# The window mask moved from matrix products to VectorE, the maximum's subtraction to GpSimd, and a new order on every engine

## The reference

```python
q, k, v = x @ Wq + bq, x @ Wk + bk, x @ Wv + bv      # 16 query heads of 8, 2 key/value heads
# keys padded by 16 on both sides; each block of 32 queries sees a span of 64 keys
scores = einsum('bhntd,bhnud->bhntu', qb, kb)         # 32 queries x 64 keys
win_mask = (u >= t) & (u < t + 32)
scores = where(win_mask, scores, -inf)
probs = softmax(scores, axis=-1)
out = einsum('bhntu,bhnud->bhntd', probs, vb)
...
x = x + out @ Wo + bo
```

## Time and profile before

| | us |
|---|---|
| median of 3 runs | 632.43 (631.92 to 635.89) |
| the profiled execution itself | 634.98 |
| its span, from the first instruction to the last | 633.2 |
| mean granted clock of TensorE, of full speed | 0.981 |
| TensorE busy | 589.3, 93% of the span |
| VectorE busy | 516.8, 82% |
| ScalarE busy | 359.4, 57% |
| GpSimd busy | 302.8, 48% |

### The profile page before, as it was taken

How to read it: one execution, slowest core, us unless ns; L and a number is a source line. 1 busy time by engine, 2 the same in 40 slices (tenths; PEclk the granted TensorE clock), 3 DMA queues, 4 the chain that set the end, 5 groups by cost and what they waited for, 6 DMA issues and landing times.

```text
span 633.2 us, 17191 instructions
## 1 busy us (share of the span) xinstructions
PE 589.3 (93%) x6484; PEld 358.4 (57%) x6484; DVE 516.8 (82%) x1195; ACT 359.4 (57%) x539; POOL 302.8 (48%) x584
## 2 busy tenths in 40 slices
PE   3866889889999999999999999999999999999896
PEld 3523354536656565555566565655555665656664
DVE  6498889898989889898989898898989898884340
ACT  1323537265757666574757576665747575756452
POOL 4021444472827274564728272745647282617342
PEclk9979798989999999999999999999999999999999
DMA  8201010101010101101010101011010101000001
GB/s 312 66 20 42 7 40 9 35 3 26 19 44 19 39 21 23 38 13 48 4 44 19 42 19 40 23 29 32 11 44 8 43 19 43 5 15 18 2 18 34
DMA packets 29458, 21.14 MB, mean 33 GB/s; under 512 B 8128, under 2 KB 25152, under 8 KB 29376
## 3 DMA queue, kind: packets, MB, share of 16 engines
q1 hardware_dynamic: 26928, 15.82, 10.2%
q10 hardware_dynamic: 2448, 4.22, 1.8%
HBM read 9.53 MB, written 4.19 MB: 22 GB/s over the span
## 4 chain that ended last, share of the span: by engine, by line
PE 85%; DVE 7%; POOL 2%; issue 2%; DMA 2%; ACT 1%; SPq 1%; ACTq 0%; DVEq 0%; POOLq 0%
PE ring L448 18%; PE ring L460 18%; PE ps_o L433 10%; PE ps_s L416 8%; PE ring L390 7%; PE ring L471 5%; PE ring L491 4%; PE ps_s L411 3%; PE ring L528 3%; PE ring L499 2%; PE ring L480 2%; PE ring L505 2%; DMA up_s<-in_up_m 1%; PE ring L548 1%; PE ring L517 1%
## 5 line engine op out<-in xcount | busy, mean ns | idle before, releaser
L709 ACT ACTIVATE probs_t<-shifted_t 128x1024 f32<-128x1024 f32 x64 | 67.4, 1054 | 53.7 <-DVE shifted_t L905 26.6
L326 POOL TENSOR_SCALAR rv_F<-mv_F 128x4 f32<-128x4 f32 x16 | 3.6, 226 | 183.2 <-DVE norm L941 161.0
L893 DVE TENSOR_REDUCE rowmax<-ps_s 128x16 f32<-128x1024 f32 x64 | 77.0, 1203 | 10.3 <-PE ps_s L416 10.1
L898 DVE TENSOR_TENSOR shifted<-ps_s,rowmax 128x1024 f32<-128x1024 f32 x64 | 78.4, 1225 | 7.0 <-DVE rowmax L893 0.5
L905 DVE STREAM_TRANSPOSE shifted_t<-shifted 128x1024 f32<-128x1024 f32 x64 | 79.1, 1236 | 0.7 <-issue 0.2
L433 PE MATMUL ps_o<-probs_t,vx 32*32 32x256 f32 x2048 | 70.8, 384 | 3.4 <-DVE vx L988 1.7
L448 PE MATMUL ring<-xT_F,w1b 128*128 128x512 f32 x128 | 70.3, 654 | 0.4 <-ACT xT_F L694 0.4
L416 PE MATMUL ps_s<-kx,q_t 64*32 64x512 f32 x1024 | 70.5, 621 | 0.0
L448 PE MATMUL ring<-xT_G,w1b 128*128 128x512 f32 x128 | 66.1, 605 | 0.7 <-ACT xT_G L694 0.7
L460 PEld LDWEIGHTS ring<-w,hid_F 128*128 128x128 f32 x512 | 58.4, 192 | 7.0 <-issue 7.0
L460 PE MATMUL ring<-w,hid_F 128*128 128x128 f32 x512 | 61.4, 278 | 0.6 <-ACT hid_F L702 0.5
(11 more groups left out here) (116 smaller groups left out, 1126.9 us busy)
## 6 DMA issues: line engine op xcount, KB each, us to landing
kx<-kv_t SPq DMA_DIRECT2D x128, 40.0 KB, 2.1
x_P<-in_x SPq DMA_DIRECT2D x16, 256.0 KB, 2.8
out_x<-x_G SPq DMA_DIRECT2D x16, 256.0 KB, 2.5
vx_t<-kv_t SPq DMA_DIRECT2D x128, 8.0 KB
up_s<-in_up_m ACTq DMA_DIRECT2D x7, 256.0 KB, 8.6
down_s<-in_down_m ACTq DMA_DIRECT2D x7, 256.0 KB, 8.6
later<-in_later_c SPq DMA_DIRECT2D x1, 648.0 KB, 9.4
u_t<-in_w_exp_t ACTq DMA_DIRECT2D x1, 258.0 KB, 5.7
```

Of the source, the lines that this page charges most:

```text
L709: nc.scalar.activation(probs_t[:, j % 2].rearrange("p k h u t -> p (k h u t)"), shifted_t[:, j % 2].rearrange("p k h u t -> p (k h u t)"), ...
L893: nc.vector.tensor_reduce(rowmax[:, j], s, AX_X, ALU.max).then_inc(vec.sem, 1)
L898: nc.vector.tensor_tensor(shifted[:, j % 2], ps_s[:].rearrange("p k (h u) -> p k h u", u=SPAN), m, ALU.subtract).then_inc(drained["S"].sem, 1)
```

## The change

1. **Mask.** The mask products and their bf16 tables are gone; the scores' products start their banks themselves. VectorE's `add_mask` adds the mask table (band, 64 numbers a partition, repeated over 16 heads) while it reads ps_s, writes the new tensor masked (two buffers) in SBUF and thereby frees ps_s. `row_max` then takes the maximum of masked.
2. **Subtraction.** GpSimd's `subtract_max` takes the maximum from masked and writes shifted, four times a group, 1024 elements a partition each. It waits for the maximum and for the transpose that last read the buffer. The block transposes wait for it.
3. **x in two buffers.** x_P and xb_P exist twice, and `load_x` waits for the group before the last.
4. **Tables.** `ready(function)` applies Gelu or Exp to one number into an unused place ahead of the first real use, in front of the waits of that use: four per steady turn (Gelu before F.up3's and before G.up3's, Exp before probs 2 and before L.k0's parts).
5. **Waits.** A table COVERED names 72 pairs of products or banks for which `drained_by` and `free` issue no wait any more; some 34 of them belong to products of every group.
6. **Order.** Every engine's turn is rewritten, with new banks and lags; TURNS is NG + 10 in place of NG + 12. P.xT comes at lag 4 and G.down at lag 10 (before: 7 and 12).

The diff, cut to its core:

```diff
-FIRST = [("ident", P), ("spread", WIN), ("band", SPAN), ("wq", P), ("wkv", 2 * KV * HD), ("bq", 1), ("bkv", 1)]
+FIRST = [("ident", P), ("band", SPAN), ("wq", P), ("wkv", 2 * KV * HD), ("bq", 1), ("bkv", 1)]
...
+        masked = sb("masked", [P, 2, KV, HPK, SPAN])
...
-                sp.wait_ge(normed.sem, normed.after(g - 1, "P.xn"))
-                sp.wait_ge(biased.sem, biased.after(g - 1, "P.xb"))
-                sp.dma_start(xs["P"][:], x_v[g]).then_inc(x_in.sem, 16)
+                sp.wait_ge(normed.sem, normed.after(g - 2, "P.xn"))
+                sp.wait_ge(biased.sem, biased.after(g - 2, "P.xb"))
+                sp.dma_start(x_of(g, "P")[:], x_v[g]).then_inc(x_in[g % 2], 16)
...
+            def subtract_max(g, j):
+                pool.wait_ge(vec.sem, vec.after(g if j >= 2 else g - 1, f"W.tr{(j - 2) % 4}"))
+                pool.wait_ge(vec.sem, vec.after(g, f"W.max{j}"))
+                m = rowmax[:, j].rearrange("p (k h a) -> p k h a", k=KV, a=1).to_broadcast([P, KV, HPK, SPAN])
+                nc.gpsimd.tensor_tensor(shifted[:, j % 2], masked[:, j % 2], m, ALU.subtract).then_inc(subtracted.sem, 1)
...
+            def drained_by(g, name, user):
+                own = drained[BANK[name]]
+                if (user, name) not in COVERED:
+                    pe.wait_ge(own.sem, own.after(g, name))
...
-                for i in range(4):
-                    for a in range(KV):
-                        half = slice(HPK * HD * a, HPK * HD * (a + 1))
-                        nc.tensor.matmul(ps_s[32 * i:32 * i + 32, a], spreadb[half], bandb[half],
-                                         start=True, stop=False, skip_group_check=True)
...
-                            start=False, stop=True, skip_group_check=True)
+                            start=True, stop=True)
...
+            def ready(function):
+
+                i = next(place)
+                nc.scalar.activation(unused[:, i:i + 1], half[0:1, 0:1], function)
...
-            def shift_by_max(g, j):
+            def add_mask(g, j):
+                if g == 0:
+                    dve.wait_ge(first_in, 16)
+                dve.wait_ge(subtracted.sem, subtracted.after(g if j >= 2 else g - 1, f"W.sb{(j - 2) % 4}"))
                 dve.wait_ge(product.sem, product.after(g, f"W.S{j}"))
...
+                nc.vector.tensor_tensor(
+                    masked[:, j % 2].rearrange("p k h u -> p (k h) u"), ps_s[:].rearrange("p k (h u) -> p (k h) u", u=SPAN),
+                    band.rearrange("p (a u) -> p a u", a=1).to_broadcast([P, HEADS, SPAN]), ALU.add
+                ).then_inc(drained["S"].sem, 1)
+
+            def row_max(g, j):
+                dve.wait_ge(subtracted.sem, subtracted.after(g - 1, f"W.sb{j}"))
+                dve.wait_ge(drained["S"].sem, drained["S"].after(g, f"W.S{j}"))
+                nc.vector.tensor_reduce(rowmax[:, j], masked[:, j % 2].rearrange("p k h u -> p (k h) u"), AX_X, ALU.max
+                                        ).then_inc(vec.sem, 1)
```

More of the change, by code:

```diff
@@ L234, in window_and_linear_attention_with_butterfly_ffn @@
         biased = Count(sem("biased"), BIASED)
-        x_in = Count(sem("x_in"), [("P.x", TRANSFERS["P.x"])], 16)
+        x_in = [sem(f"x_in{i}") for i in range(2)]
         kx_in = Count(sem("kx_in"), [("P.kx", TRANSFERS["P.kx"])], 16 * HPK)
@@ L589, in turn @@
[L589 to L601 removed]
+                if t == 6:
+                    up_stage(4, "a")
@@ new lines, in turn @@
+                for g in due(t, 6):
+                    scores(g, 2)
+                if t == 6:
+                    up_stage(5, "a")
+                for g in due(t, 7):
+                    heads_transposed(g)
+                if t == 6:
+                    up_stage(2, "b")
+                for g in due(t, 5):
+                    attention_kv(g)
+                if t == 5:
+                    up_stage(1, "a")
+                for g in due(t, 8):
+                    norm_transposed(g, "L", "F")
@@ new lines, in turn @@
+                if t == 7:
+                    up_stage(6, "a")
+                for g in due(t, 7):
+                    project(g, "W", o_wt, wo_s)
+                for g in due(t, 8):
+                    linear_kv_rows(g, 0)
+                    linear_kv_rows(g, 1)
+                if t == 6:
+                    up_stage(3, "b")
+                for g in due(t, 6):
+                    scores(g, 3)
+                for g in due(t, 8):
+                    linear_q(g)
+                if t == 5:
+                    down_stage(0)
@@ new lines, in turn @@
+                for g in due(t, 5):
+                    gelu(g, "F", 0)
+                    gelu(g, "F", 1)
+                    gelu(g, "F", 2)
+                for g in due(t, 4):
+                    ready(ACT.Exp)
+                    probs_out(g, 2)
+                if t == 4:
+                    up_stage_out(5, "b")
+                for g in due(t, 7):
+                    copy_out(g, "G.xT", x_t["G"][:], *UPS["G"])
+                for g in due(t, 6):
+                    copy_out(g, "L.oT", o_lt[:], "L.proj")
@@ L1030, in turn @@
+                if t == 3:
+                    up_outer_stage(1)
+                for g in due(t, 4):
+                    phi_q_made(g)
+                for g in due(t, 2):
+                    scores_transposed(g, 1)
+                    add_mask(g, 3)
+                for g in due(t, 4):
+                    linear_state_out(g)
+                for g in due(t, 6):
+                    residual(g, "G", "G.down", "L")
                 for g in due(t, 0):
```

543 lines of the change are left out of this document (258 added, 285 removed), and 36 rows, old and new, of tables (COVERED, PRODUCTS, VECTOR).

## The result

| | before | after |
|---|---|---|
| median, us | 632.78 (4 runs, 631.92 to 635.89) | 617.33 (4 runs, 616.30 to 618.24) |
| profiled execution, us | 634.98 | 618.24 |
| its span, us | 633.2 | 616.4 |
| mean granted clock of TensorE over the span | 0.981 | 0.992 |

The ratio of after to before is 0.9747, 95% interval 0.9709 to 0.9785: 15.45 us faster. 619.3 had been forecast. Of all the executions reported here one, of the kernel before with touches (984.55 us at a mean granted clock of 0.562), was in a slow state and is in no ratio.

The account below looks back on a forecast made before the run. TensorE was taken to bound the kernel, busy 34.83 of 34.83 us per group. Mask -14.1, GpSimd waiting +4 and start -3 sum to -13.1: 621.9 for the profiled execution, 619.3 us as median, range 604 to 640.

Parts of the forecast that it names:

- Mask products, −14.1: TensorE's scores: dropping eight mask products per tile saves 0.22 us on each of 64 tiles, 14.1 us.
- which is also what I expect without the mask: TensorE's scores take 0.97 us to the next product's start, with or without mask products ahead, out of 1.20 per tile.
- The lower bound: Mask gain on TensorE if scores now pay a 0.1 us array-shape change: 0.12 us a tile, 7.7 us.
- Order and waits of TensorE, 0: 18 runs of one array shape per group before and after, met waits cost nothing: 0; upper bound 28 us.
- Rival 1: More comes back on TensorE: the mask's full busy time counts or dropped waits are worth something; 605 us, chance 0.20.
- by my walk two would: VectorE's four head outputs per group: two would dodge GpSimd's two-operand passes, which hold them; 2.3 us a group charged.
- Rival 3: VectorE becomes the bound through head outputs held by GpSimd's passes: 652 us, chance 0.14.
- GpSimd, new waiting, +4: Normalisations queued behind GpSimd's subtractions make TensorE wait 0.3 us a group over some 13 steady groups: 4 us lost.
- Start and end, −3: Filling and draining: P.kv and scores of group 0 start 6 us sooner, half is kept, 3 us saved; bounds -6 and +5.
- Tables, 0: ScalarE's touches move table loads into its waits; ScalarE doesn't end last, so 0, with 1.28 us sooner freed banks as cover.
- Keys with 1.8 us to spare, x, SyncE, 0: Key loads take 7.4 us of 9.2 between scores 3 and scores 0; the second x buffer also brings 0.
- Rival 2: Mask, maximum, subtraction and transpose handoffs between VectorE and GpSimd eat the gain: 631.3 us, chance 0.16.

Follow-up runs that it names:

- the kernel with the moments ahead: The changed kernel with VectorE's W moments of group 0 moved ahead of the first outer butterfly stage of the up weights: 616.5 us, ratio 0.9746 to the kernel before.

## Why the prediction was right, and which terms were not

**What bounds it.** Right, before and after: TensorE is busy in the whole period in both, and 11.2 of the 15.45 us follow its period.

**Mask products, −14.1.** The step "which is also what I expect without the mask" is the one that was mis-sized. The scores took 0.97 behind mask products and 1.02 without them. By 64 tiles that is 11.5 where 14.1 stood, and the run with the products put back gives 11.2 to 11.5. The lower bound had named this: the mask products could hide a change of shape that the scores would then pay. About half of the 0.1 feared there came (0.05), if that is what it is. The Trainium skill (TensorEngine Tiling (Array Packing), section "Tiling Modes") states that a change of tiling mode drains TensorE; it gives no price. The runs show 0.05 us more on the first products of the new shape, but not that a drain is what it consists of.

**Order and waits of TensorE, 0.** The sum is right, but it is made of two small terms that cancel. The 34 waits are worth 0.07 us a group. And the new order has 19 runs of one shape a group, where the prediction counted 18 in both: the scores stand beside P.kv and L.kv once each in the old order and beside neither in the new one, where L.kv stands beside weighted values 0. With the mask put back, the dropped waits still gone and the same instructions as before, the period is 0.02 longer than before. So one more change of shape costs about 0.09 us, an estimate from 0.02 + 0.07, near the 0.1 that the prediction read for one. Nothing is left for its upper bound of 28 us. Rival 1 falls with it, as its other half, the mask's full busy time of 26.7 us, came to 11.5.

**VectorE.** Right in its parts: 1204 ns for the mask addition (1225 forecast), 1208 for the maximum (1200). 32.4 busy had been forecast and 30.05 came, mostly because the holds went the other way: 2.3 us a group had been charged and 0.2 came. "by my walk two would" dodge a subtraction was the wrong step: all four do. The mean head output fell from 496 to 343 ns, so (343 − 293) x 64 = 3.2 us are lost where 13 were. Rival 3 had the hold right, as the run with doubled subtractions shows, and its occasion wrong: the order keeps the two apart. Its further step, that VectorE then becomes the bound, was not seen even there. By the Trainium skill (SBUF — State Buffer, section "Who interferes with whom") the two share a port under a lock; the trace of the doubled subtractions agrees, with 41 of the 44 head outputs that met one taking longer than a free one.

**GpSimd, new waiting, +4.** The subtraction took 1.90 and not 2.5, since a second operand repeated along the row is cheaper here than a full one (2.37). GpSimd has 26.4 of 34.13 where 28.8 was forecast. But the 4 us of steady waiting would hardly have come at 28.8 either: at 28.37 the period was the same. The charge of "0.3 us a group of new waiting" measured 0: TensorE has no gap between 150 and 500 us.

**Start and end, −3.** The 4 to 5 us that came are near this 3 by luck, as "I keep half" was wrong in its parts and one part wasn't in the sum at all.

The head start alone is worth 6.7 us, in full and as idle time: P.kv starts at 13.96 in place of 19.48, the scores at 25.43 in place of 28.99.

The part that the prediction didn't have is the clock. In windows of 5 us it lay below 1.00 at 25 to 50, 60 to 75 and 95 to 105 us before, and at 60 to 75 and 85 to 95 after. In windows of 0.50 TensorE is at the lower of its two levels, 1.2 GHz; what that costs is seen in F.up of group 0 in the rows of the kernel with the moments ahead (four products in 3.78 us, against 1.98 in after). In after the clock fell within TensorE's wait of 6.78 us for xn_W (0.95 from 60 to 65 us, 0.50 from 65 to 70). In before it fell at the 2.1 us wait for the keys or just behind (0.94 from 25 to 30, 0.72 from 30 to 35); no run isolates that cause. With the same instructions as before, the kernel with the mask put back is busy for 584.7 us against 589.3, and its clock is 1.00 in all windows up to 60 us. So 4.6 of the 6.8 us between these two profiled spans (633.2 and 626.4) are products that ran shorter, which I put down to the clock. It isn't the head start that brings this: with the first transposes held back the clock is 1.00 in all windows up to 70 us too. The mean clock also differs between executions of one kernel, and the time with it: before took 631.39 us at 0.988 and 636.96 at 0.976.

Against both stands the longer filling. In these two profiled executions 6.7 + 4.6 − 6.8, that is 4.5 us, went to it; by the idle time it is 6.5, as the gaps of TensorE, with the time ahead of its first product, add up to 39.8 us after and 40.3 before, though holding the head start back alone adds 7. Both are estimates, and no run isolates it. The execution of before that was profiled is also one of its longer ones, so at the medians, where 5.2 us lie outside the steady periods, the clock's share is likely below 4.6. (The 4 us left beside the steady periods in the result and these 5.2 differ by the spread of the runs: the kernel before has medians from 632.36 to 633.63.)

**Tables, 0.** Right for the old order ("ScalarE doesn't end last": 0.9985), wrong as a statement on the new one: the touch before L.k0 is a cover that this order needs, worth 7 us. The prediction had named the sooner freed banks as cover, but hadn't asked what it costs if that cover is gone. It didn't move the forecast, as the change has both.

**Keys with 1.8 us to spare, x, SyncE, 0.** Right: no steady gap ahead of the scores.

**The sum.** Forecast −14.1 + 4 − 3 = −13.1; measured −11.5 + 0 − 4 = −15.5 (15.45 by the medians). Three terms were off by 2.6, 4 and 1, of mixed sign, and the total by 2.4. The forecast of 619.3 was near because the errors partly cancelled, not because each was small, and the last term hides three larger ones: −6.7, up to −4.6, and 4.5 to 6.5 against them. Rival 2 (the handoffs eat the gain) is what happens in the old order as placed here, 675.71, and with a GpSimd that is nearly full, 653.0.

## What to carry to other kernels

When one engine is full in every period, price a removed instruction by the distance of starts with and without it, and leave a bit for what it hid (here 0.05 of 0.23). Work moved to an idle engine was free here only with an order that keeps the handoff off the queues it feeds: the same move was 42 us slower in the old order, 41 slower without GpSimd and 15 faster with both. An edit that looks free in one order can be a cover that another order needs, so test it in the order in which it ships. And before the gain of a new start is put down to its schedule, compare TensorE's busy time for the same instructions: here a good part of it was the granted clock.

## What the runs showed that was not expected

- GpSimd's pass of two operands and 1024 elements a partition took 1.90 us with a second operand repeated along the row, and 2.37 us with a full one. VectorE took 1.226 us (median) for the former, and no run has it with the latter. The Trainium skill (GPSIMD Engine Reference, section "Performance versus the Vector engine") has GpSimd about 2 times slower in elementwise work; here it is 1.55 times with the repeated operand, and the full one on GpSimd takes 1.9 times VectorE's 1.226.
- A table load costs its 1.28 us and nothing beside it here: 59 loads have 1.1 us of idle time ahead of them in all, and the touch starts 0.01 us behind the load (292.27 + 1.28 to 293.56). The Trainium skill (ScalarE: Activation LUTs, section "What ACT_TABLE_LOAD costs") adds a drain of about 1.38 us to each switch; these traces don't show it.
- A delay of 1.28 us on an engine that is two thirds full cost the kernel 0.63 us a period (34.76 to 34.13): 0.36 as a gap before G.down, the rest as longer products around it.
- P.kv of group 0 runs slow behind a wait though the profile has a granted clock of 1.00: its two products take 1.91 us at 13.96 in after, and 1.05 at 19.48 in before, where TensorE had been at work since 11.98. It isn't the nearness to the start: with the first transposes held back, behind a wait of 7.32 us, they take 1.91 at 20.78 too. So a little of the 6 us by which P.xT was moved ahead (18.06 to 12.10) was given back at once: from P.xT to P.kv it is 1.86 us after and 1.42 before.
- 6.8 us of a start that was held went into the total in full, although a wait of 6.78 us for xn_W lay behind it, which might have taken it up and was just as long in both.
